# Mamba and soft-MoE kernel: softplus written twice by ScalarE, and the running sums of the steps taken per chunk from the PSUM copy

## The reference, cut to what matters

```
delta = softplus(delta @ dt_proj_w.T + dt_proj_b)          # per channel, per time
dA = delta * A[n]
dA_cum = exp(flip(cumsum(flip(shift(dA)))))                # sum of all later steps
xs = cumsum(delta * u * B[n] * dA_cum) / (dA_cum + 1e-12)  # for 16 states n
y  = sum_n xs * C[n] ;  y + u * D ;  times silu(res)
```

## Time and profile before

| what | value |
|---|---|
| median of 3 runs | 6041.84 us (6036.67 to 6042.24) |
| the profiled execution: span | 6039.5 us |
| busy: PE, DVE, ACT, POOL | 84%, 79%, 68%, 74% of the span |
| the 16 sequences, 102 to 4950 us: DVE, POOL, PE, ACT busy | 4427, 4453, 4021, 3934 us of 4848 |

### The profile page before, as it was taken

How to read it: one execution, slowest core, us unless ns; L and a number is a source line. 1 busy time by engine, 2 the same in 40 slices (tenths; PEclk the granted TensorE clock), 3 DMA queues, 4 the chain that set the end, 5 groups by cost and what they waited for, 6 DMA issues and landing times. The chain is left out here.

```text
span 6039.5 us, 50725 instructions
## 1 busy us (share of the span) xinstructions
PE 5055.7 (84%) x14640; PEld 2557.8 (42%) x14640; DVE 4751.8 (79%) x4049; ACT 4091.2 (68%) x6429; POOL 4464.2 (74%) x2134
## 2 busy tenths in 40 slices
PE   5888887888887878888888888888888888999988
PEld 2333333333333333333333333443333434565566
DVE  5998989998989998999999999899999871222233
ACT  3878787878887878787878887878788863111100
POOL 3999999999999999999898999998989970000000
PEclk9999899999999999999999999999999999999988
DMA  2444344444443444444443444343434432323265
GB/s 71 129 127 132 123 129 125 130 123 128 128 132 123 129 127 126 126 126 129 124 132 124 128 127 133 126 128 124 132 124 128 130 106 83 101 76 101 80 228 203
DMA packets 555572, 755.29 MB, mean 125 GB/s; under 512 B 124059, under 2 KB 272411, under 8 KB 553245
## 3 DMA queue, kind: packets, MB, share of 16 engines
q1 hardware_dynamic: 555293, 752.04, 39.8%
HBM read 662.04 MB, written 89.82 MB: 124 GB/s over the span
## 5 line engine op out<-in xcount | busy, mean ns | idle before, releaser
L628 POOL TENSOR_TENSOR g_ring<-dtu,b_ring 128x1024 f32<-128x1024 f32 x1026 | 2514.5, 2454 | 362.2 <-DVE e_ps L976 335.1
L976 DVE TENSOR_TENSOR_SCAN e_ps<-e_ps,g_ring 128x1024 f32<-128x1024 f32 x1024 | 2345.2, 2290 | 168.3 <-ACT e_ps L782 156.2
L782 ACT ACTIVATE e_ps<-dt,a_neg 128x512 f32<-128x512 f32 x2050 | 1398.5, 682 | 721.7 <-DVE v_own L998 484.6
L1141 PE MATMUL y_ps<-v_ring,ident 128*128 128x512 f32 x3088 | 1632.2, 638 | 231.9 <-DVE res_gate L959 193.8
L637 POOL TENSOR_TENSOR v_ring<-z_ring,c_ring 128x1024 f32<-128x1024 f32 x768 | 1822.2, 2373 | 0.0
L792 ACT ACTIVATE f_ring<-rsum,consts,a_neg_half 128x512 f32<-128x512 f32 x2050 | 1645.8, 803 | 0.8
L989 DVE SCALAR_TENSOR_TENSOR z_ring<-f_ring,e_ps 128x1024 f32<-128x1024 f32 x768 | 934.9, 1217 | 49.7 <-issue 1.7
L1141 PEld LDWEIGHTS y_ps<-v_ring,ident 128*128 128x128 f32 x3088 | 592.6, 206 | 884.9 <-issue 815.3
L1141 PE MATMUL y_ps<-v_own,ident 128*128 128x512 f32 x1028 | 535.4, 616 | 0.0
L1074 PE MATMUL side<-u,conv_diag 128*128 128x512 f32 x1088 | 491.8, 595 | 23.2 <-ACT disp_ring L743 18.7
L1251 ACT ACTIVATE x_act<-x_gate,x_bg 128x512 f32<-128x512 f32 x128 | 87.9, 687 | 570.8 <-PE x_gate L1283 570.8
(11 more groups left out here) (134 smaller groups left out, 5206.1 us busy)
## 6 DMA issues: line engine op xcount, KB each, us to landing
b_ring<-bc_scr SPq DMA_DIRECT2D x1027, 256.0 KB, 3.7
c_ring<-bc_scr SPq DMA_DIRECT2D x1025, 256.0 KB, 3.4
pT_scr<-rowT_ring SPq DMA_DIRECT2D x136, 256.0 KB, 4.0
m_pT<-pT_scr SPq DMA_DIRECT2D x16, 2048.0 KB, 8.7
sT_scr<-sT_ring SPq DMA_DIRECT2D x272, 64.0 KB, 2.9
x_xT<-sT_scr SPq DMA_DIRECT2D x16, 1024.0 KB, 9.2
eo_scr<-x_eo SPq DMA_DIRECT2D x32, 512.0 KB, 5.1
m_eo<-eo_scr SPq DMA_DIRECT2D x16, 1024.0 KB, 11.0
```

Of the source, the lines that this page charges most:

```text
L628: pool.tensor_tensor(g_ring[:, k], dtu[d][:], both(b_ring[:, k:k + 1]), ALU.mult).then_inc(g_done, 1)
L782: act.activation(e_ps[:, i % 2, h], dt[d][:, h], ACT.Exp, scale=a_neg[:, d, c, n:n + 1]).then_inc(e_done, 1)
L976: dve.tensor_tensor_scan(e, e, g, 0.0, ALU.mult, ALU.add).then_inc(scan_done, 1)
L1141: pe.matmul(y_ps[:, t % 2], ident[:], v, start=(t % (TILES // PAIRS) < 2), stop=True, skip_group_check=True).then_inc(v_used, 1)
```

## The change

The softplus of both banks is written first into `dt` as before, and then a second time in place, into the two PSUM banks. VectorE takes the sums from the banks, one scan of 511 elements per chunk, the second input a row of ones in SBUF; only these scans free the banks. GpSimd and ScalarE wait for semaphores that fit (`dt_done`, `cut_done`). In the timetable the `dt` slots count 4 in place of 2 (`HOLD`). By `slot_tiles` this moves slots between the fixed ones: pair 2 to turns 36 and 37 and the slots after it up to `conv1_1` one turn later (`in0_1` and `conv0_0` two: `in0_0` stays at 38, `in0_1` 38 to 40, `conv0_0` 42 to 44, `rows2` 50 to 51, `conv1_0` and `conv1_1` 52, 53 to 53, 54); pair 3 to 66 and 68, `slots2` 68 to 70, `slots3` 71 to 72, `cols4` 73 to 74; pair 4 to 97 and 99, `slots4` 100 to 102, `slots5` 102 to 104, `x1_0` 104 to 106, and the eight slots after it by one turn or not at all. Pair 1 keeps its turns.

```diff
-HOLD = {..., "dt0": 2, "dt1": 2, "in0": 3,
+HOLD = {..., "dt0": 4, "dt1": 4, "in0": 3,
...
-        border = sb("border", [P, 2 * L - 1])
+        ones = sb("ones", [P, L - 1])
...
             def dtu_of_pair(at, s):
-                for j in (s - 1, s):
-                    pool.wait_ge(side_free[at.bank(j)], at.freed(j))
+                pool.wait_ge(dt_done, at.pair(s))
...
             def cut_chunks(at, s):
-                pool.wait_ge(rsum_done, at.pair(s))
+                for j in (s - 1, s):
+                    pool.wait_ge(side_free[at.bank(j)], at.freed(j))
                 pool.wait_ge(dtu_done, at.pair(s))
...
-                        act.activation(dt[d][:, 0], side[:, at.bank(s - 1)], ACT.Softplus).then_inc(
-                            side_free[at.bank(s - 1)], 1)
-                        act.activation(dt[d][:, 1], src, ACT.Softplus).then_inc(free, 1)
+                        both_banks = (side[:, at.bank(s - 1)], src)
+                        act.activation(dt[d][:, 0], both_banks[0], ACT.Softplus)
+                        act.activation(dt[d][:, 1], both_banks[1], ACT.Softplus).then_inc(dt_done, 1)
+                        for bank in both_banks:
+                            act.activation(bank, bank, ACT.Softplus).then_inc(plus_done, 1)
...
                 if i % N == 0 and h == 0:
-                    act.wait_ge(rsum_done, b * (NDIR * PAIRS) + (gi // N + 1))
+                    act.wait_ge(cut_done, b * (NDIR * PAIRS) + (gi // N + 1))
...
-                        for j in (s - 1, s):
-                            dve.wait_ge(side_free[at.bank(j)], at.freed(j))
...
-                        dve.tensor_tensor_scan(out, data, turn, 0.0, ALU.add, ALU.mult).then_inc(rsum_done, 1)
+                        dve.memset(rsum[d][:, :, L - 1:L] if d == 0 else rsum[d][:, :, 0:1], 0.0)
+                        for h, j in enumerate((s - 1, s)):
+                            dve.wait_ge(plus_done, 2 * at.pair(s) - 1 + h)
+                            bank, sums = side[:, at.bank(j)], rsum[d][:, h]
+                            out, data = (sums[:, 0:L - 1][:, ::-1], bank[:, 1:L][:, ::-1]) if d == 0 else (
+                                sums[:, 1:L], bank[:, 0:L - 1])
+                            dve.tensor_tensor_scan(out, data, ones[:], 0.0, ALU.add, ALU.mult).then_inc(
+                                side_free[at.bank(j)], 1)
```

More of the change, by code:

```diff
@@ L132, in timetable @@
     return [(name[:-1].rstrip("_"), int(name[-1])) for name in order.split()]
-HOLD = {"out": 3, "res": 4, "conv0": 4.5, "conv1": 4.5, "x0": 3, "x1": 3, "dt0": 2, "dt1": 2, "in0": 3,
+HOLD = {"out": 3, "res": 4, "conv0": 4.5, "conv1": 4.5, "x0": 3, "x1": 3, "dt0": 4, "dt1": 4, "in0": 3,
         "xnT": 2, "rows": 3, "cols": 4, "rowsT": 2, "colsT": 2, "slots": 3}
@@ L353, in sequence_stage @@
         half_done = sem("half_done")
-        rsum_done, dtu_done, cut_done = sem("rsum_done"), sem("dtu_done"), sem("cut_done")
+        dt_done, plus_done, dtu_done, cut_done = sem("dt_done"), sem("plus_done"), sem("dtu_done"), sem("cut_done")
         e_done, f_done, g_done, scan_done, z_done = (
@@ L826, in _ @@
             dve.memset(cut, CUT)
-            dve.memset(border[:, 0:L - 1], 1.0)
-            dve.memset(border[:, L - 1:L], 0.0)
-            dve.memset(border[:, L:], 1.0)
+            dve.memset(ones[:], 1.0)
             dve.memset(slope[:, 0], -0.5)
```

## The result

The changed kernel takes 6125.4 us (median of 4 runs, 6120.3 to 6125.7) beside 6040.3 us of the kernel before: 1.013 times as long, 95% interval 1.011 to 1.015. It is slower, by 85 us; 6114 was predicted, range 6015 to 6160. The profiled execution has a span of 6123.8 us, 84.3 more than the one of before.

What follows compares the result with a forecast made beforehand. The path was taken to run through VectorE, with gaps from ScalarE and TensorE. -68 + 16 x (2 + 8.5 - 1.8) = +71, one more in the prologue, gave a 6111.5 us span, so 6114 us, range 6015 to 6160.

Steps and rivals of the forecast that it cites:

- The path runs through VectorE: Whole sequence: a us on VectorE counts in full unless a gap from ScalarE or TensorE takes it up.
- No collision, 2.28 us per pair: New sum scans on VectorE: 1.14 us per chunk, 2.28 per pair, no collision with GpSimd's products.
- Pair 1: First sum-scan pair of each sequence: 11 long scans of 6.2 us avoided, 68 us gained, nothing beyond.
- Pair 2: Second pair, even to odd turn, in0_0 waiting for the first sum scan: +2 us a sequence, ends -1.1 and +3.0.
- half-clock branch: At pair 2, the four matmuls before ScalarE's copy take 3.75 us instead of 1.88, making +0.7 instead of -1.1.
- Pair 3: Third pair, odd to even turn: y_gate delayed 6.3 us, clock 2.2 more; +8.5 a sequence, ends +6.3 and +8.8.
- Pair 4: Fourth pair, even to odd turn: VectorE's gap shrinks from 2.44 to 0.7 us; -1.8 us a sequence taken.
- The sum: All pairs: -68 + 16 x (2 + 8.5 - 1.8) = +71 us, one more in the prologue.
- The signs: Profile marks of being right: 1.15 us scans, gate waits 5 to 7 us, recurrence's ScalarE waits moved to pair 3, clock 0.50.
- The absorbed bank wait: Rival at TensorE's turns 70 to 73: y_gate finds its matmuls done, pair 3 only +2.2, 5950 us; chance 0.16.
- the full clock: Rival: TensorE stays at full clock, lateness after pairs 2 and 4 small, 6042 us; chance 0.12.
- the collision: Rival: new scans collide too, as ones and output are in SBUF; 68 us stay, 6200 us; chance 0.04.

Runs made afterwards that it cites:

- e4: Changed kernel with both chunks' sums read from dt in SBUF in place of the PSUM banks: 6248.9 us.
- e12: The kernel before, unchanged, profiled again: span 6015.1 us.
- e2: Changed kernel with seven matmuls of zeros into y_ps ahead of slots2, while TensorE waits for the bank: 6104.5 us.
- e10: Changed kernel with sums one turn earlier (RSUM_LAG 3), plus three matmuls of zeros ahead of slots2 and three ahead of in0_0: 5948.3 us.
- e6: The kernel before with only the new timetable (HOLD 4 in place of 2): 6029.1 us, ratio 0.9997 to the kernel before.
- e11: The kernel before with the new timetable and the scan one turn earlier, still one softplus and a scan over SBUF: 5933.8 us, ratio 0.9836.
- e8: Changed kernel with sums one turn earlier and slots2 to cols5 placed behind the gate: 6016.6 us.
- e9: The kernel before with only the scan one turn earlier (RSUM_LAG 3), old timetable: 5955.2 us, ratio 0.9867.

## Why the prediction was right, step by step

- **The path runs through VectorE.** Right: it waited for GpSimd once, at the start, in the changed kernel too, and the step table follows what VectorE's queue holds.
- **No collision, 2.28 us per pair.** Right in kind; measured 2 x 1.21 (starts 1.13 apart). e4 shows the cause.
- **Pair 1, 68 us and nothing besides.** Measured 16 x 4.38 = 70. The price of 6.2 us for a long scan held in e12 as well.
- **Pair 2, +2, upper end +3.0.** Measured +2.58 and +1.12 behind it, 3.7: the term was under-sized, and its upper end too low. The half-clock branch of the working was the true one: it gave 9.6 us from the recurrence scan of step 20 to that of step 21 and +0.7 for the place, and the traces have 9.8 and +0.8. The slots behind it were counted as "a turn later"; that the column reduction of step 21 (`cols0`) would wait as well, 1.76 us a sequence, was left out. The term is short by 1.7 us a sequence, 27 us of the time, and the one that was clearly off.
- **Pair 3, +8.5, ends +6.3 and +8.8.** Measured +7.5: gap 3.36 (3.45), TensorE idle 8.04 (about 8), gate waiting 6.0. Over-sized by 1.0, of which the clock is 0.6: it costs 1.6 us (e2), not 2.2, as the clock came back after the first sixteen matmuls. The other 0.4 was not traced to a place.
- **Pair 4, -1.8.** Measured -2.80 and +0.90 behind it: -1.9.
- **The sum** of +8.7 became 7.5 + 3.7 - 1.9 = 9.3, the gain of pair 1 was 70 where 68 was set: +79 in the place of +71. Outside the steps 1 us was set and 5 came, so 6125 against 6114. That it is so close is partly luck: pair 2 was 1.7 us too small and pair 3 1.0 too large.
- **The signs.** The scans, the gate (6.0 us once per sequence, 96 in all) and the distance from pair 1 to pair 1 (307.1 to 309.0 us, about 307 said) came as named; the granted clock around `slots2` was 0.59, 0.50 said. One did not: the recurrence's waits for ScalarE did not move away from pair 2. Its 3.43 us in step 20 became 3.97 in step 21; only pair 4's 2.42 went.
- **The rivals.** The absorbed bank wait fell with the gate's 96.3 us; the full clock with the 0.59 after 8 us of idling; the collision with 1.22 us as the longest scan.
- **The two rules of the Trainium skill.** SBUF — State Buffer, "Who interferes with whom": that the loser of the shared port waits for one instruction would have left pair 1 a gain of 26 us; 70 came, and scans of 10.1 us in the earlier trace rows and 8.05 in e4 (511 elements) are beyond one product. TensorE: Matmul & The Clock Gate, "What's actually happening": the rule that the idle array has half the clock the runs bear out, with 1.6 of pair 3's 7.5 us (e2), and at pair 2 2.4 us (e10, in the version with the earlier scan).

Not shown: why VectorE loses several products in a row in some sequences and one in others. It was not tried to make the second softplus pay by freeing the banks at once, since the scans need them.

## What to carry to other kernels

A scan is as cheap as the place it stands in: with the new timetable and one softplus, steps 34 to 37 take 18.20 us with the scan behind the recurrence (e6) and 16.13 with it in the gap one turn earlier (e11). That one number moved the changed kernel by 121 us and the kernel before by 82 (95 with the new timetable), where the change moved it by 85. Before an engine is spared a collision by keeping a shared buffer longer, follow the queue of whoever refills that buffer up to the next barrier: here a PSUM bank held 7 us longer (at pair 3 from ScalarE's first softplus, done at 1513.97, to the end of the first sum scan at 1520.90) came back as 8 us of idle TensorE and 6 us at the gate. And where TensorE must wait, count the next few microseconds of its work at half clock, as after the 4.18 and 8.04 us here, or give it something to do.

## What the runs showed of the hardware that I had not expected

- A VectorE scan with two SBUF inputs can lose to several GpSimd products in a row (511 elements: 1.19 to 8.05 us, 1023: 2.28 to 11.9 us). While the scan of 10.03 us in the earlier trace rows lasts (1034.98 to 1045.01), GpSimd in the kernel before does three products one after another at their usual length, and then waits for the scan:

```profile
1036.09 2.34 POOL L637 TENSOR_TENSOR v_ring<-z_ring,c_ring 128x1024 f32<-128x1024 f32 x1
1038.39 2.18 POOL L610 TENSOR_TENSOR dtu<-dt,u 128x1024 f32<-128x1024 f32 x1
1040.53 2.35 POOL L628 TENSOR_TENSOR g_ring<-dtu,b_ring 128x1024 f32<-128x1024 f32 x1
1045.10 0.20 POOL L617 TENSOR_TENSOR dt<-consts 128x1 f32<-128x1 f32 x1 [2.22 <-DVE rsum L917]
```

- How many scans are long is decided anew in each execution: 11 and 7 in two executions of the same kernel, whose single runs spread over 55 us. The kernels whose scans take one input from PSUM spread over 3 to 9 us, one of them (e8) over 14 by a single run.
- Seven matmul calls of zeros, 6.2 us of TensorE, made the kernel 21 us faster; six calls in the better version 56 us. At a granted clock of 1.00 in place of 0.59 the same sixteen matmuls took 2.05 us instead of 3.62.
- Taking the scan one turn earlier in the kernel before left 2 long first scans of 16, where that kernel's two traces have 11 and 7, without changing its inputs (e9; 1 in e11). That is one trace each; why was not tested.
